# Spare expert tiles read in place by register, half 1 routed ahead of the experts, and another order on ScalarE, GpSimd and VectorE

## The chip, the cores and the metric

The kernel runs on one core of one Trainium2 chip. The metric is the device time in microseconds (us) of one execution; its median over 3 runs was 405.51 (404.76 to 406.37). Engines are named PE (TensorE), DVE (VectorE), ACT (ScalarE), POOL (GpSimd) and SP (SyncE, which here only issues transfers).

## The reference

Input: x of 4 x 256 rows of 256 numbers, and a context of 4 x 256 rows of 64. Four blocks are added to x in turn, each gated by a tanh:

```python
x = x + tanh(g_xattn[0]) * attn0(layernorm(x), ctx)     # softmax over 256 of a normalised similarity
x = x + tanh(g_ffn[0])   * ffn0(layernorm(x))           # router: the best 1 of 32 experts per row
x = x + tanh(g_xattn[1]) * attn1(ctx, layernorm(x))     # sigmoid of the top 76 of 256, made symmetric
x = x + tanh(g_ffn[1])   * ffn1(layernorm(x))           # top 8 of 64 experts, and one shared expert
```

In ffn0 each of the 32 experts has one ternary weight matrix of 256 x 256, masked by its own 0/1 mask, and a row gets only the output of the expert that its router picked. In ffn1 all 64 experts are computed for all rows and weighted by a row of W that is zero outside the best 8.

## The kernel before

The 1024 rows lie as T = 8 tiles of 128 rows; tiles 0 to 3 are half 0, tiles 4 to 7 half 1. Each engine has its instructions written out by hand in one order, and semaphores tie them together. The order of those lists is what the change moves.

**attn0.** attend(h) on DVE adds the softmax rows to X and asks POOL for the roots of the variances (rsqrt(r), r counts the requests); norm_rows on ACT writes the normalised rows (f16 high part to rows16, f32 to XN) and low_rows on POOL the low part. router_x and router (PE) give the router's logits, choose (DVE) the expert of each row.

**ffn0, routed.** Rows are put into tiles of CAP = 32 rows of one expert: 32 own tiles, one for each expert, and SPARE = 15 spare tiles for experts with more than 32 rows in a half. ranks, owners and owners_of (PE) with assign_spares, assign_owners, assign_slots and set_owners (DVE) give every row its slot, and spare_e the expert of each spare tile. scatter(h) (POOL, 4 indirect transfers) sends the rows to memory, load_rows(h) (ACT's queue) reads them back in slot order. There are 12 groups of four tiles, in 6 pieces p. For a piece PE transposes (routed_x), ACT copies (routed_rows), PE multiplies (experts) with m16, the masked weights, that DVE makes in eight mask_weights; ACT copies the result (expert_rows) and stores it (store_rows). In experts the four tiles of a group have a column group of the array each: a matmul is 128 rows deep, 32 columns wide and streams 256. Pieces 4 and 5 are the spare tiles. Their weights are copies: load_spares(h) on SP reads an expert number into a register and moves 128 KB within the core's memory, 15 times a half.

gather(h) (POOL) brings each row's output back to Z, weigh_rows (ACT) multiplies by the router's weight wtop, which weights_of_rows(h) on DVE makes from router_exp(h) on ACT, and add_rows (POOL) adds to X.

**attn1.** The search for the 76 largest of each row of SIM runs on DVE the whole time: find(n) is n steps, each a MAX8 or a MATCH_REPLACE8, 19 steps a tile (need_of), strung in between all other DVE work. adjacency(t) follows the 19 steps of tile t and needs tanh_rows on ACT. symmetric(0, k) on PE makes the symmetric matrix of two tiles and needs both adjacencies. rows_stats and rows_ask(h) (DVE), rsqrt (POOL), rows_affine (DVE), mix_rows (ACT), rows_mix (DVE) and rows_moments (DVE) with another rsqrt lead to rows_normalise; prep_x3t transposes it on PE and prep_rows copies it on ACT.

**ffn1.** shared_step and then 2 x 32 passes of pair_step and down, each for two experts. SP loads the weights of pair q to one of two stages (load_pair, which waits until lo_ready says that the stage was read), high_half on ACT makes their f16 high part, low_half on POOL the low part. Pairs 0 to 7 are prepared ahead of the loop. keep_busy are fills: matmuls on ones whose result nobody reads.

The expression that the change replaces in experts is this one (lines 985 to 990):

```python
e = 4 * (2 * p + k) + j
w = m16[:, e, c, :] if e < E0 else wov[h][min(e - E0, SPARE - 1)][:, c, :]
last = mm(ps_y[p % 2][CAP * j:CAP * (j + 1), k * D:(k + 1) * D],
          xT[:, h, 2 * p + k, c, s, CAP * j:CAP * (j + 1)], w,
          start=(i == 0), stop=(i == 2 * C - 1), skip_group_check=True)
```

## Time and profile before

| | us |
|---|---|
| median of 3 runs | 405.51 |
| the profiled execution | 406.02 |
| its span, from first to last instruction | 404.3 |
| PE busy (of 2419 matmuls) | 358.7 |
| DVE busy | 272.6 |
| ACT busy | 181.1 |
| POOL busy | 163.0 |
| span up to the first shared projection | 123.4 |

Busy time is the time in which an engine works at something; its share says nothing of who waits for whom. The profile also lists who waited for whom, and the instructions of an engine in order of time: these are the views to read for a change of order.

### The profile page before, as it was taken

Reading aid. Unit: us, or ns where it says so; the run is one execution under the profiler, and the core shown is the slowest. Engines: PE = TensorE matmul, PEld = TensorE weight load, DVE = VectorE, ACT = ScalarE, POOL = GpSimd, SP = SyncE. Lnnn points to the kernel's source line nnn. Section 1 sums busy time; section 2 is a strip of 40 time slices with the busy share of each in tenths; the row PEclk is TensorE's granted clock in tenths of the full one; section 3 lists DMA queues with packets and bytes.
Section 4 is the critical chain, followed back from the end, with each engine's and each line's share of the span. In section 5 each row is a group of like instructions: output and inputs, shape, how many; then the busy total and the mean of one; then the engine's idle time right before and its main releaser. Section 6 shows DMA issues by size and latency. Waiting matters only on the chain. (4 is left out here: it accounts for less than half of the span.)

```text
span 404.3 us, 7694 instructions
## 1 busy us (share of the span) xinstructions
PE 358.7 (89%) x2419; PEld 217.4 (54%) x2419; DVE 272.6 (67%) x711; ACT 181.1 (45%) x354; POOL 163.0 (40%) x180
## 2 busy tenths in 40 slices
PE   8987928643977899999899999969999999999995
PEld 2755426312644365546466666645665656656563
DVE  3999896999376585999784484557555555555454
ACT  3477736624744446544645446533323233332331
POOL 6937542437551349978699677220000000000000
PEclk9996967785999899999999999999999999999999
DMA  7899964686701444445355442004121221212211
GB/s 186 139 258 218 197 208 149 221 263 217 233 17 51 128 137 131 130 131 195 132 190 174 159 153 73 25 29 146 61 78 58 72 71 58 78 56 74 77 53 52
DMA packets 50346, 51.31 MB, mean 127 GB/s; under 512 B 6732, under 2 KB 41484, under 8 KB 50318
## 3 DMA queue, kind: packets, MB, share of 16 engines
q1 hardware_dynamic: 34430, 38.08, 30.0%
q0 software_dynamic: 9216, 6.29, 9.1%
q10 hardware_dynamic: 6672, 6.59, 5.1%
q8 instruction: 14, 0.23, 0.2%
q14 instruction: 14, 0.11, 0.1%
HBM read 44.13 MB, written 7.08 MB: 127 GB/s over the span
## 5 line engine op out<-in xcount | busy, mean ns | idle before, releaser
L1047 PE MATMUL bank<-early,gu 128*128 128x512 f16 x768 | 177.7, 381 | 3.0 <-DVE arena L1608 3.0
L1047 PEld LDWEIGHTS bank<-early,gu 128*128 128x128 f16 (+1 forms) x768 | 75.0, 98 | 83.0 <-issue 4.4
L499 ACT ACTIVATE arena<-arena 128x512 f16<-128x512 f32 (+1 forms) x66 | 41.6, 631 | 134.6 <-DVE arena L1624 133.8
L1074 PE MATMUL bank<-dp,arena 128*128 128x256 f16 (+1 forms) x768 | 94.2, 273 | 1.1 <-POOL arena L457 0.7
L1074 PEld LDWEIGHTS bank<-dp,arena 128*128 128x128 f16 x768 | 74.7, 98 | 23.5 <-POOL arena L457 2.7
L1608 DVE TENSOR_TENSOR arena<-arena,bank 128x512 f32<-128x512 f32 x64 | 43.9, 686 | 56.7 <-PE bank L1047 40.2
L457 POOL TENSOR_TENSOR arena<-arena 128x512 f16<-128x512 f32 (+1 forms) x33 | 38.3, 1161 | 51.1 <-ACT arena L499 51.1
L1624 DVE TENSOR_TENSOR arena<-arena,early 128x512 f32<-128x512 f32 x64 | 48.4, 756 | 7.5 <-DVE arena L1608 2.7
L740 ACT ACTIVATE arena<-bank 128x512 f32<-128x512 f32 (+1 forms) x66 | 38.7, 588 | 17.5 <-PE bank L1047 17.4
L406 POOL TENSOR_TENSOR gu<-stage,gu 128x512 f16<-128x512 f32 x32 | 39.0, 1219 | 7.4 <-ACT dp L499 7.4
L1634 DVE TENSOR_TENSOR arena<-arena 128x512 f16<-128x512 f32 (+1 forms) x33 | 22.8, 691 | 24.5 <-ACT arena L499 24.5
L1206 DVE MAX8 t<-work 128x8 f32<-128x256 f32 x72 | 30.7, 426 | 2.0
L795 PE MATMUL bank<-ones 128*128 128x512 f16 x97 | 26.5, 420 | 1.8 <-DVE ones L1508 1.1
L407 POOL TENSOR_TENSOR dp<-stage,dp 128x256 f16<-128x256 f32 x32 | 27.5, 859 | 0.0
L1211 DVE MATCH_REPLACE8 work<-t,work 128x256 f32<-128x256 f32 x64 | 26.1, 408 | 0.0
L499 ACT ACTIVATE gu<-stage 128x512 f16<-128x512 f32 x32 | 19.7, 617 | 0.7 <-ACT arena L499 0.5
L975 PE MATMUL bank<-gu 128*32 128x256 f16 x256 | 12.0, 344 | 7.7 <-ACT gu L499 7.7
L795 PEld LDWEIGHTS bank<-ones 128*128 128x128 f16 x97 | 9.3, 104 | 16.0 <-issue 7.4
L499 ACT ACTIVATE arena<-bank 128x512 f32<-128x512 f32 (+1 forms) x18 | 10.7, 595 | 12.9 <-PE bank L975 7.0
L399 POOL TENSOR_TENSOR rstd<-var_in,minus_half 128x4 f32<-128x4 f32 x8 | 8.2, 1026 | 18.5 <-DVE var_in L1247 17.0
L1233 DVE BATCH_NORM_STATS2 bn<-X 128x6 f32<-128x256 f32 x32 | 11.8, 413 | 5.2 <-DMA X<-in_x 5.2
L420 POOL DMA_INDIRECT routed_rows<-arena,slot x8 | 10.1, 1265 | 8.9 <-DVE slot L1397 7.1
(184 smaller groups left out, 368.6 us busy)
## 6 DMA issues: line engine op xcount, KB each, us to landing
early<-token_weights SPq DMA_DIRECT2D x126, 128.0 KB, 2.9
stage<-in_gu_t SPq DMA_DIRECT2D x32, 256.0 KB
gu<-in_masks_t POOLq DMA_DIRECT2D x16, 256.0 KB, 22.5
stage<-in_dp_t SPq DMA_DIRECT2D x32, 128.0 KB
expert_rows<-arena ACTq DMA_DIRECT2D x12, 256.0 KB
dp<-gu SPq DMA_DIRECT2D x22, 128.0 KB, 2.3
routed_rows<-arena SPq DMA_DIRECT2D x1, 1536.0 KB, 17.5
arena<-routed_rows ACTq DMA_DIRECT2D x3, 512.0 KB, 5.1
```

The costliest lines, as they stand in the source:

```text
L406: nc.gpsimd.tensor_tensor(gu16[:, q, 1, :, :], stage_gu[s], gu16[:, q, 0, :, :], ALU.subtract)
L407: nc.gpsimd.tensor_tensor(dp16[:, q, 1, :], stage_dn[s], dp16[:, q, 0, :], ALU.subtract).then_inc(lo_ready, 1)
L457: nc.gpsimd.tensor_tensor(inter16[0:m, s, 1, :], inter[0:m, s, :], inter16[0:m, s, 0, :], ALU.subtract).then_inc(ilo_ready, 1)
L499: return nc.scalar.activation(dst, src, ACT.Copy, scale=scale)
L740: nc.scalar.activation(silu[0:m, s, :], ps_gate[s][0:m, :], ACT.Silu).then_inc(silu_ready, 1)
L795: mm(dst.rearrange("p (a b) -> p a b", a=4), ones16[:, :], ones16[:, None, :].to_broadcast([P, 4, P]), start=True, stop=True)
L1047: last = mm(dst[:, :], w, x16[:, h, b, c, :], start=(k == 0), stop=(k == 3 * C - 1))
L1074: last = mm(dst, inter16[0:m, s, a, k * P:(k + 1) * P], w, start=(q is None and j == 0 and k % 2 == 0), stop=True, skip_group_check=True)
L1206: last = steps(v.max(t8[:, t, :], src))
L1211: last = steps(v.match_replace(work[:, :], t8[:, t, :], src, NEG))
L1608: v.tensor_tensor(gated[0:m, s, :], silu[0:m, s, :], up, ALU.mult).then_inc(gated_ready, 1)
L1624: v.tensor_tensor(inter[0:m, s, :], gated[0:m, s, :], row, ALU.mult).then_inc(inter_ready, 1)
```

## The change

1. **Spare tiles.** load_spares and its copies are gone. PE loads the 15 expert numbers into registers (spare_owners(h)) and takes the weights from m16 at the register's address. The rows of a spare tile are laid so that a full 128-column slice holds its 32 columns at the tile's place and zeros elsewhere (DVE writes the zeros once at the start), and all four tiles of a group add up in one accumulation over full-width matmuls (experts_spare).
2. **Half 1 sooner.** The masks are applied behind attend(1); softmax_rows(1), router_x, router, router_rows(1) and norm_rows(1) stand ahead of half 0's experts; load_rows(1) and tanh_rows(0) stand behind store_rows(0, 3), and router_exp(1) behind half 0's last store.
3. **POOL.** rsqrt(4) follows add_rows at once, gather(1) follows low_half(4), rsqrt(5) stands ahead of low_half(7), and add_rows(4 to 7) ahead of the loop; on ACT weigh_rows(4 to 7) are ahead of prep_rows(0).
4. Fills and search steps are counted anew; statistics of half 1 stand three passes earlier in the loop.

Three places of the lists. DVE, behind set_owners of half 0. L1504 and L1524 are mask_weights, the TENSOR_TENSOR into gu. Before:

```order
L1406 COPY place<-idxf 128x4
L1504 TENSOR_TENSOR gu<-gu,tern 128x4x256 x12
L1316 ISA Z,tiny<-Z,beta_sb 128x256
```

and behind attend(1) in the changed kernel:

```order
L1267 TENSOR_SCALAR var_in<-mv 128x4
L1524 TENSOR_TENSOR gu<-gu,tern 128x4x256 x6
L1361 SCALAR_TENSOR_TENSOR nmr<-mv,rstd 128x4
L1524 TENSOR_TENSOR gu<-gu,tern 128x4x256 x6
L1369 COPY lg<-bank 128x128
L1372 MAX top<-lg 128x8 x4
```

The twelve instructions moved from ahead of the second softmax to between attend(1) and choose(1), whose first row is the COPY.

ACT, at the end of half 0's experts. Before, with router_exp(1) (L606) ahead of the copies of pieces 4 and 5:

```order
L634 DMA expert_rows<-arena 128x2x256 [waits y_copied]
L606 ACTIVATE lg,tiny<-lg,tiny,rstd 128x32 [waits max_ready]
L606 ACTIVATE lg,tiny<-lg,tiny,rstd 128x32 x3
L499 ACTIVATE arena<-bank 128x512 [waits y_ready]
L634 DMA expert_rows<-arena 128x2x256 [waits y_copied]
```

and now (L594 is router_exp):

```order
L635 DMA expert_rows<-arena 128x2x256 [waits y_copied]
L603 DMA early<-routed_rows 128x4x512 [waits row_out]
L603 DMA early<-routed_rows 128x4x512 x2
L641 ACTIVATE XN<-SIM 128x1024 [waits rows_ready]
L644 ACTIVATE XN<-XN 128x1024 [waits act_step]
L487 ACTIVATE arena<-bank 128x512 [waits y_ready]
L635 DMA expert_rows<-arena 128x2x256 [waits y_copied]
L487 ACTIVATE arena<-bank 128x512 [waits y_ready]
L635 DMA expert_rows<-arena 128x2x256 [waits y_copied]
L594 ACTIVATE lg,tiny<-lg,tiny,rstd 128x32 [waits max_ready]
L594 ACTIVATE lg,tiny<-lg,tiny,rstd 128x32 x3
```

The loads of half 1, both tanh passes and two copies now stand ahead of router_exp(1).

POOL, from the fifth root on, in the changed kernel (L386 root, L393 and L394 low_half, L416 gather):

```order
L386 TENSOR_TENSOR rstd<-var_in,minus_half 128x4 [waits var_ready]
L393 TENSOR_TENSOR gu<-stage,gu 128x512 [waits hi_ready]
L394 TENSOR_TENSOR dp<-stage,dp 128x256
L416 DMA Z<-expert_rows,slot 128x256 [waits y_out]
L416 DMA Z<-expert_rows,slot 128x256 x3
L393 TENSOR_TENSOR gu<-stage,gu 128x512 [waits hi_ready]
L394 TENSOR_TENSOR dp<-stage,dp 128x256
L393 TENSOR_TENSOR gu<-stage,gu 128x512 [waits hi_ready]
L394 TENSOR_TENSOR dp<-stage,dp 128x256
L386 TENSOR_TENSOR rstd<-var_in,minus_half 128x4 [waits var_ready]
```

Before, three low_half stood ahead of the first of these roots and one between the two, and the gather behind both.

The diff, cut:

```diff
 dp16 = sb("dp16", [P, PAIRS, 2, D], F16)
+spare_zero = dp16[:, PAIRS // 2:, :, :].rearrange("p a b c -> p (a b c)")
+spare_x = spare_zero.rearrange("p (k c s n) -> p k c s n", k=4, c=C, s=2)
+own_x = spare_zero.rearrange("p (a j n) -> p a j n", j=4, n=P)[:, :, :, 0:CAP]
...
 rows16 = arena[:, 0:4096].rearrange("p (k s n) -> p k s n", k=T, s=2)
-more = arena[:, 4096:8192].rearrange("p (j c o) -> p j c o", c=C, o=D)
-wov = [[dp16[:, PAIRS // 2 + j, :, :] for j in range(SPARE)],
-       [more[:, j, :, :] if j < 8 else dp16[:, j + 1, :, :] for j in range(SPARE)]]
...
-    def load_spares(h):
...
-        sp.wait_ge(owner_set, h + 1)
-        sp.wait_ge(mask_ready, MB)
-        for j in range(SPARE):
-            e = sp.value_load(spare_e[0:1, h, j:j + 1], min_val=0, max_val=E0 - 1)
-            sp.dma_start(wov[h][j], m16[:, bass.ds(e, 1), :, :].rearrange("p e c o -> p (e c) o")
-                         ).then_inc(wov_in[h], 16)
...
     load_pair(3)
-    load_spares(0)
-    load_pair(4)
-    load_pair(5)
-    load_spares(1)
-    for q in range(6, 8):
+    for q in range(4, 8):
...
         add_rows(t)
-    for q in range(4, 7):
-        low_half(q)
     rsqrt(4, HT)
+    low_half(4)
+    gather(1)
+    low_half(5)
+    low_half(6)
+    rsqrt(5, HT)
     low_half(7)
-    rsqrt(5, HT)
-    gather(1)
+    for t in range(HT, T):
+        add_rows(t)
...
         low_step(n, (n + 1) % 2)
-        if n == 10:
+        if n == 8:
             rsqrt(6, HT)
-        if 4 <= n < 4 + HT:
-            add_rows(n)
...
             act.wait_ge(y_ready, PIECES)
-        if q == 9:
+        if q == 10:
...
+    def spare_rows(h, p):
...
+        if h == 0:
+            act.wait_ge(spare_set, 1)
+        else:
+            act.wait_ge(y_ready, p + 1)
+        a = 4 * C * (p - E0 // 8)
+        copy(own_x[:, a:a + 4 * C, :, :], ps_xt[p % 2].rearrange("p (a j n) -> p a j n", j=4, n=CAP)
+             ).then_inc(xt_copied, 1)
...
         act.wait_ge(xt_ready, PIECES * h + p + 1)
+        if p >= E0 // 8:
+            spare_rows(h, p)
+            return
...
     scale_rows(1)
+    router_exp(0)
+    softmax_rows(1)
     sim1_rows(1, 0, 1)
-    router_exp(0)
     high_half(2)
-    tanh_rows(0)
...
     load_rows(0)
-    softmax_rows(1)
+    router_rows(1)
+    norm_rows(1, 4, 5, 6, 7)
...
     store_rows(0, 1)
-    router_rows(1)
-    norm_rows(1, 4, 5)
...
     store_rows(0, 2)
-    norm_rows(1, 6, 7)
...
     store_rows(0, 3)
-    router_exp(1)
+    load_rows(1)
+    tanh_rows(0)
...
     store_rows(0, 5)
+    router_exp(1)
...
     high_half(4)
-    high_half(5)
-    load_rows(1)
-    weigh_rows(0, 1, 2, 3)
...
     store_rows(1, 1)
+    weigh_rows(0, 1)
...
     store_rows(1, 2)
+    weigh_rows(2, 3)
...
     store_rows(1, 3)
-    high_half(6)
...
     store_rows(1, 5)
+    high_half(5)
+    high_half(6)
...
     high_half(7)
+    weigh_rows(4, 5, 6, 7)
...
             high_half(n + 4)
-        if n == 3:
-            weigh_rows(HT, HT + 1)
-        if n == 5:
-            weigh_rows(HT + 2, HT + 3)
-        if n == 6:
+        if n == 4:
             tanh_rows(1)
-        if n == 14:
+        if n == 12:
...
+    owner = []
...
+    def spare_owners(h):
...
+        pe.wait_ge(owner_set, h + 1)
+        owner[:] = [pe.value_load(spare_e[0:1, h, j:j + 1], min_val=0, max_val=E0 - 1) for j in range(SPARE)]
...
+    def experts_spare(h, p):
...
+        n = PIECES * h + p
+        pe.wait_ge(xt_copied, n + 1)
+        for k in range(2):
+            first = 2 * p + k - E0 // 4
+            for i in range(8 * C):
+                j, c, s = i // (2 * C), i // 2 % C, i % 2
+                e = owner[min(4 * first + j, SPARE - 1)]
+                last = mm(ps_y[p % 2][:, k * D:(k + 1) * D], spare_x[:, first, c, s, 96 * j:96 * j + P],
+                          m16[:, bass.ds(e, 1), c, :].rearrange("p e o -> p (e o)"),
+                          start=(i == 0), stop=(i == 8 * C - 1))
+        last.then_inc(y_ready, 1)
...
             pe.wait_ge(y_copied, n - 1)
-        if p == E0 // 8:
-            pe.wait_ge(wov_in[h], 16 * SPARE)
+        if p >= E0 // 8:
+            experts_spare(h, p)
+            return
...
                 for j in range(4):
-                    e = 4 * (2 * p + k) + j
-                    w = m16[:, e, c, :] if e < E0 else wov[h][min(e - E0, SPARE - 1)][:, c, :]
                     last = mm(ps_y[p % 2][CAP * j:CAP * (j + 1), k * D:(k + 1) * D],
-                              xT[:, h, 2 * p + k, c, s, CAP * j:CAP * (j + 1)], w,
+                              xT[:, h, 2 * p + k, c, s, CAP * j:CAP * (j + 1)], m16[:, 4 * (2 * p + k) + j, c, :],
...
     router(0)
-    sim1(1, 0, 1)
-    keep_busy(4, bank[0][:, :])
+    keep_busy(8, bank[0][:, :])
...
     owners_of(0)
-    keep_busy(36, bank[0][:, :])
+    sim1(1, 0, 1)
+    spare_owners(0)
+    keep_busy(20, bank[0][:, :])
+    router_x((2, 3))
+    keep_busy(4, bank[0][:, :])
+    router(1)
+    keep_busy(4, bank[0][:, :])
...
     routed_x(0, 2)
+    ranks(1)
...
     routed_x(0, 3)
-    router_x((2, 3))
+    owners(1)
...
     routed_x(0, 4)
-    router(1)
-    experts(0, 3, 0)
-    ranks(1)
-    experts(0, 3, 1)
+    owners_of(1)
+    experts(0, 3)
     routed_x(0, 5)
-    owners(1)
-    experts(0, 4, 0)
-    owners_of(1)
-    experts(0, 4, 1)
+    experts(0, 4)
     experts(0, 5)
+    spare_owners(1)
...
     experts(1, 5)
-    keep_busy(10, bank[0][:, :])
     symmetric(0, 0)
+    keep_busy(24, bank[0][:, :])
...
     v.memset(ones16[:, :], 1.0).then_inc(ones16_set, 1)
+    v.memset(spare_zero.bitcast(F32), 0.0).then_inc(spare_set, 1)
...
     choose(0)
-    find(2)
+    find(1)
...
     set_owners(0)
-    for m in range(2, MB):
-        mask_weights(m)
...
     weights_of_rows(0)
-    find(4)
+    find(6)
     attend(1)
+    for m in range(2, 5):
+        mask_weights(m)
+    attended(1)
+    for m in range(5, MB):
+        mask_weights(m)
+    choose(1)
     find(3)
-    attended(1)
-    find(6)
-    choose(1)
-    find(2)
...
         seen += 1
-    thresholds(HT * need_of - used[0] - 8)
+    thresholds(HT * need_of - used[0] - 20)
...
     rows_ask(0)
-    thresholds(2)
+    thresholds(4)
     rows_affine(0)
+    thresholds(10)
...
         find(4 if n in (2, 3, 4) or n > 8 else 3)
-        if 7 <= n < 7 + HT:
-            rows_stats(n - 3)
-        if n == 10:
+        if 4 <= n < 4 + HT:
+            rows_stats(n)
+        if n == 8:
             rows_ask(1)
-        if n == 13:
+        if n == 11:
```

## Rows read from the trace of the kernel before

**Rows 1.** The page: busy tenths of PE in 40 slices; the threshold search's MAX8
```profile
PE   8987928643977899999899999969999999999995
...
L1206 DVE MAX8 t<-work 128x8 f32<-128x256 f32 x72 | 30.7, 426 | 2.0
```

**Rows 2.** PE in order of time: start us, duration us, line, tiles, xcount, [idle before <-releaser]
```profile
97.89 1.90 PE L975 MATMUL bank<-gu 128*32 128x256 f16 x32 [6.25 <-ACT gu L499]
...
107.33 1.06 PE L975 MATMUL bank<-dp,gu 128*32 128x256 f16 x32 [0.22 <-ACT gu L499]
...
119.08 1.40 PE L1006 MATMUL bank<-ident,XN 128*128 128x128 f32 x8 [1.90 <-DVE XN L1283]
...
123.42 1.46 PE L1033 MATMUL bank<-early,shared 128*128 128x512 f16 x6
```

**Rows 3.** What DVE waited for: us in total, times, longest
```profile
DVE mix L1441 <- POOL rstd L399: 5.9, 1, 5.9
...
DVE lg L1349 <- PE bank L908: 3.7, 1, 3.7
...
DVE X L1452 <- PE bank L996: 2.0, 2, 1.1
...
DVE spares L1367 <- PE bank L925: 1.4, 1, 1.4
```

**Rows 4.** DVE in order of time, 44 to 78 us
```profile
44.20 11.02 DVE L1504 TENSOR_TENSOR gu<-gu,tern 128x1024 f16<-128x1024 f16 x12
...
62.81 0.08 DVE L1211 MATCH_VALUE_LOAD work<-t,work 128x8 f32 x1
...
70.92 0.29 DVE L1349 COPY lg<-bank 128x128 f32<-128x128 f32 x1 [3.68 <-PE bank L908]
...
77.27 0.17 DVE L1397 SCALAR_TENSOR_TENSOR slot<-place,rank_off 128x4 uint32<-128x4 f32 x1
```

**Rows 5.** PE in order of time, 35 to 71 us
```profile
35.05 3.75 PE L860 MATMUL bank<-early 64*128 64x256 f32 x8 [1.60 <-DVE Z L1307]
...
42.87 7.94 PE L795 MATMUL bank<-ones 128*128 128x512 f16 x36
...
65.10 0.61 PE L896 MATMUL bank<-ident,X 128*128 128x128 f32 x4
...
68.96 1.92 PE L908 MATMUL bank<-router_c,xn_t 128*128 128x32 f32 x16
```

**Rows 6.** Sequencers of SP and PE by line: duration ns min/median/max
```profile
L284 SPq TENSOR_LOAD <-spare_e x30: 13/273/957, 55.3 to 97.4; - x30
L284 SPq FUSED_REGOPS  x30: 5/152/177, 55.8 to 97.7; - x30
...
L1047 PEldq FUSED_REGOPS  x240: 46/46/60, 278.5 to 392.1; - x120
```

**Rows 7.** POOL in order of time, 77 to 111 us
```profile
77.72 1.03 POOL L420 DMA_INDIRECT routed_rows<-arena,slot  x1 [3.43 <-DVE slot L1397]
...
100.70 1.16 POOL L406 TENSOR_TENSOR gu<-stage,gu 128x512 f16<-128x512 f32 x1
...
109.83 1.05 POOL L399 TENSOR_TENSOR rstd<-var_in,minus_half 128x4 f32<-128x4 f32 x1
```

**Rows 8.** ACT in order of time, 44 to 78 us
```profile
44.70 1.05 ACT L640 ACTIVATE XN<-SIM 128x1024 f32<-128x1024 f32 x1
...
52.60 1.52 ACTq L615 DMA_DIRECT2D arena<-routed_rows  x3
...
77.18 0.40 ACT L606 ACTIVATE lg<-lg,tiny,rstd 128x32 f32<-128x32 f32 x1
```

**Rows 9.** PE's idle times within the first passes of the pair loop
```profile
174.61 2.75 PE L1047 MATMUL bank<-early,gu 128*128 128x512 f16 x12 [0.33 <-DVE arena L1608]
...
182.03 1.48 PE L1074 MATMUL bank<-dp,arena 128*128 128x256 f16 x12 [0.69 <-POOL arena L457]
...
196.69 2.75 PE L1047 MATMUL bank<-early,gu 128*128 128x512 f16 x12 [1.37 <-DVE arena L1608]
```

3 lines of the change are left out of this document (1 added, 2 removed).

## The prediction

> **What bounds the kernel now.** I read the page first. Its busy tenths of PE [rows 1] fall into two parts: from slice 14 on (some 138 us) PE is at 9 almost without a break, in 66 passes of the pair loop; before that it is often at 3 to 7. So time can be won in the first 123 us, ahead of the first pass, and in the few idle times within the passes. The last row of PE ahead of the loop is the shared projection at 123.42; it needs the transposes at 119.08, and those waited for DVE's XN [rows 2]. Following DVE back, its waits [rows 3] name what it stood for: 5.91 us for GpSimd's fifth root (mix), 3.68 for the second router logits (lg), 1.98 for the symmetric tiles, 1.40 for the first ranks. Their sum is 12.97 us. Apart from these DVE worked without a pause from 38.8 to 117, mostly in the threshold search; half 0's last adjacency, and through it the symmetric tiles, need all of its 76 search steps of four tiles. I call this DVE's line: both kernels do the same DVE work between 38.8 and the transposes, so the transposes move by what the idle time changes. PE's wait of 6.25 at 97.89 [rows 2] is not on that line: ACT stood in front of gathered rows, and half 1's experts still ended at 108.4, ahead of the need.
>
> **The early part.** Ranks of half 0 no longer stand behind sim1 and its fills, so most of the 1.40 goes (0.4 stays), and one search step fewer stands ahead (0.45, a MAX8 [rows 1]): DVE is free at 42.75 where it was at 44.20 [rows 4]. Then come the rows of the second softmax, search and attend(1), which filled 55.2 to 62.8 [rows 4]: 7.6, with two more search steps, 8.6; then six masks, 11.02 [rows 4]. DVE reaches the choice of half 1 at 42.75 + 8.6 + 11.0 + 0.1 = 62.5, where it was at 70.92 [rows 4]: 8.4 sooner.
>
> **The register loads.** Nothing in this trace loads a register on PE. The nearest row is SP's: a load 0.273 at the median and 0.152 of register work behind it [rows 6], with a check of 0.02 some 0.443, fifteen of them 6.6 us. Below, PE's sequencer can run ahead of the array: its 240 register operations in the loop cost 46 ns each [rows 6] and PE shows no idle time for them, which would make the loads free. Above, SP's longest load was 0.957 [rows 6], 1.13 with the rest, so fifteen take 17 us. I take 6.6, half of it beside sim1 where sim1 stands in front, and all of it in the open for half 1. So for half 0: sim1 starts at 41.3 and takes 3.75 [rows 5], to 45.1; the loads end near 50.4; 20 fills at 0.22 each (36 took 7.94 [rows 5]), some of them at half clock, take 6.0, to 56.4; two transposes with their copies and the second router took 65.10 to 70.88 with expert work between [rows 5], 5.1 without it: logits at 61.5. That is 1.0 ahead of DVE's need at 62.5, so the wait of 3.68 goes. **This is the first place where it can turn**: each us later than 62.5 is a us of DVE.
>
> **Slots of half 1.** From the choice to the slots took 70.92 to 77.4 [rows 4], 6.5. One search step more (0.5), ranks behind the first experts (0.45) and 0.2 at the owners make 7.65: slots at 70.2, 7.2 sooner. Idle 0.65.
>
> **The new wait on DVE.** This speaks against the change. DVE takes the weights of half 1 right behind its owners, near 71.3, and for that it needs router_exp(1). ACT now does that behind load_rows(1) (which waits for the scatter), tanh_rows(0) and the last two expert copies. From the slots: 0.3 to the start of the scatter; four issues near 1.0 with 0.3 between and the last end, 5.0 [rows 7]; 1.5 until ACT sees them (the first scatter ended at 51.1, its loads went out at 52.60 [rows 8]); 1.52 for three load issues; 2.1 for two passes like the 1.05 one; 1.15 for two copies with stores; 1.65 for four exponentials of 0.40 [rows 8]. That is 13.2: 83.4, and DVE waits 12.1 us. Nothing else is behind it but the search, which is what the end needs. So idle time becomes 0.4 + 0.65 + 12.1 + 0.95 (one symmetric tile pair) = 14.1 where it was 12.97: **+1.1 us**. GpSimd's 5.91 [rows 3] does vanish: the root no longer waits for a weight half (109.83 [rows 7] against a request at 103.6), and ten search steps stand where DVE stood. The gain and the new wait nearly cancel.
>
> **ACT ahead of the transposed rows.** weigh_rows(4 to 7) now stand in front of prep_rows(0), behind high_half(7), whose stage is free only when GpSimd has done low_half(5), and that is behind the second gather. From the fifth request: root 1.05, low_half(4) 1.75 (100.70 to 102.45), gather 4.9 as the scatter, low_half(5) 1.75 [rows 7], the load 3.5 (estimate), high_half 1.0, four weighings 1.8: 15.8. DVE's way from the same request to the first transposes is 1.95 + 0.5 + 5.35 + 0.95 + 0.9 + 3.9 = 13.55, and 0.7 more to their copy, 14.25. So ACT is **1.5 us** late; 0 at the low end, with a load of 2 us, and 2.5 at the high end. mix_rows(0) behind high_half(6) costs another 0.2.
>
> **Spare tiles.** A piece of 32 matmuls in four column tiles took 1.06 us [rows 2]. Full width they stream 256 columns one after another; twelve of 512 columns take 2.75 in a pass [rows 9], 0.11 for 256, so 3.6 us, 2.5 more for each of two pieces a half. Half 0's end stays ahead of ACT's scatter wait (cost 0); half 1's experts end near 105.3 instead of 108.4, its rows are out near 109.7, just when GpSimd is done with low_half(4): cost 0, with no slack. The Trainium skill (TensorEngine Tiling (Array Packing), Theoretical Speedup) gives a dimension of at most 32 up to a factor of 4, which speaks against giving up the tiles. By it a piece would take 4.2 us, half 1 would end 1.4 later and the whole would be 1.4 us more than my sum; the trace shows 3.4 (3.6 against 1.06), so it agrees in direction and stays under the page's bound. The removed transfers appear in none of DVE's waits [rows 3]: 0. The memset fits into DVE's first wait for x: 0.
>
> **The loop.** The idle times of 0.33 and 0.69 [rows 9] came in passes where DVE had statistics on top of four searches, and GpSimd had add_rows and the root; both move to lighter places or ahead of the loop: **-1.0**, between 0 and -2.6. The 1.37 stands behind mix_rows(1) on ACT and only moves with it.
>
> **The sum.** +1.1 + 1.5 + 0.2 - 1.0 = +1.8 us. The profiled execution took 406.02, so 407.8; the median of the runs is 0.5 below it, which gives **407.3 us**. About 0.5% (2 us) is what a measurement of this kernel can tell from no change.
>
> **The rivals.** (1) Slower: PE's register loads don't run beside sim1. They then end at 51.7, the array has been idle so long that more fills go at half clock (7.3), logits come at 64.1. The choice is 1.6 late and the later steps on PE 1.2: +2.8 on my sum, 410. Were a load as long as SP's longest, logits would be at 74 and the time near 419. It decides as soon as the loads end after 51.5. For it: the long load in [rows 6]. Against: PE hides its register work in the loop. Chance 0.18. (2) Slower: half 1's experts end late, because loads, fills and full-width pieces add up, and the fifth normalisation's root, now behind gather(1) on GpSimd, waits for it. Each us after 109.7 costs one: with 3 us, 410. For it: the gather starts with no slack in my working; against: ACT may be through sooner, as I count the loads in full. Chance 0.11. (3) Faster: the new wait is shorter (scatter and landing 1.5 less), the stage of pair 7 lands in 2 us, and all three idle times in the loop go (-1.6): 1.8 - 1.5 - 1.5 - 1.6 = -2.8, 402.7. For it: DVE stands still while GpSimd writes the scatter, and the root has no weight half in front. Against: each of the three must come true. Chance 0.21. My forecast has 0.50.
>
> **The numbers.** Range 402.5 to 412.5, from rival 3 to a little beyond rivals 1 and 2; about a tenth is left out on either side (above, the long register load). My own case reaches from 405 to 409.5, and three tenths of it are over 2 us slower: 0.15, with both slower rivals 0.44. Rival 3 gives 0.20 for faster by over 0.5%, a little of it ending within. That leaves 0.36 for within.
>
> **What would show it.** DVE waiting some 12 us for ACT's router_exp at the reciprocal behind the owners; no wait for logits or for the fifth root; transposes of XN between 119 and 122; ACT's copy of them behind weigh_rows; spare pieces near 3.6 us; no idle 0.69 in the loop. I am wrong if that DVE wait is under 9 us, if PE's loads take over 8 us or under 2, or if the first shared projection is ahead of 123.

## The result, and the profile after

| | kernel before | changed kernel | ratio, with its 95% interval |
|---|---|---|---|
| timed first | 405.94 (404.76 to 406.8) | 418.9 (418.38 to 420.86) | 1.0314 [1.0256, 1.0371] |
| once more, on another chip | 408.85 (405.35 to 411.63, 24 runs) | 414.38 (413.13 to 417.04, 9 runs) | 1.0125 [1.0089, 1.0162] |

The change is slower: by 3.1% where it was timed first, by 1.2% where it was timed beside its variants. Both agree in direction and disagree in size. All variants below are ratios to the kernel before, timed beside them, and so belong with the second row. The kernel before varies there by some 1.5% from run to run, so differences under half a per cent are read from traces, not from times.

Below are the trace of the first timing (span 419.1) and that of the repeat (span 411.3). First the busy tenths and clock of the changed kernel's page:

```profile
PE   8896668919967889999999999969999999999995
...
PEclk9969569968978889999999999978999999999999
```

A slice is 10.5 us here and 10.1 in the kernel before. Counted from 1, PE is steadily at 9 from slice 16 on (157 us), in [rows 1] from slice 15 (141 us). Ahead of it the clock is below 9 in slices 3, 5, 6, 9, 10 and 12 to 15, and then once more in slices 27 and 28 (272 to 293 us), around the turn of the halves. What DVE waited for from 39 to 132 us, first timing and then repeat (36 to 130 us):

```profile
DVE tiny L1432 <- ACT lg L594: 13.6, 1, 13.6
DVE X L1472 <- PE bank L1014: 3.2, 1, 3.2
DVE lg L1369 <- PE bank L906: 2.2, 1, 2.2
DVE spares L1387 <- PE bank L923: 1.6, 2, 1.4
```

```profile
DVE tiny L1432 <- ACT lg L594: 12.7, 1, 12.7
DVE lg L1369 <- PE bank L906: 2.1, 1, 2.1
DVE spares L1387 <- PE bank L923: 1.6, 2, 1.4
DVE X L1472 <- issue: 1.6, 1, 1.6
DVE bn L1253 <- POOL X L438: 0.6, 1, 0.6
```

Against [rows 3]: the 5.9 us for GpSimd's root are gone, 12.7 to 13.6 us for half 1's router exponentials on ACT have come, the wait for logits shrank but did not go. PE in order of time, first timing:

```profile
47.48 1.91 PE L858 MATMUL bank<-early 64*128 64x256 f32 x4
56.34 3.88 PE L793 MATMUL bank<-ones 128*128 128x512 f16 x9 [6.95 <-issue]
...
76.68 7.15 PE L952 MATMUL bank<-gu,dp 128*128 x64
92.28 3.59 PE L793 MATMUL bank<-ones 128*128 128x512 f16 x8 [8.45 <-issue]
...
132.02 0.66 PE L1024 MATMUL bank<-ident,XN 128*128 128x128 f32 x4 [1.85 <-DVE XN L1303]
...
138.12 2.45 PE L1051 MATMUL bank<-early,shared 128*128 128x512 f16 x6 [1.22 <-DVE early L1484]
```

The two idle times of 6.95 and 8.45 us are the register loads. The transposes stand at 132.02 (119.08 in [rows 2]) and the shared projection at 138.12 (123.42), at half clock: 2.45 us for what took 1.46. The sequencer's loads for half 0:

```profile
L941 PEldq TENSOR_LOAD <-spare_e x15: 293/301/493, 46.4 to 55.7; - x15
L941 PEldq FUSED_REGOPS  x15: 146/146/165, 47.0 to 56.1; - x15
```

From the first to the last there are 9.3 us over 14 steps: 0.66 us each, although load, register work and check last 0.465 together.

**The start.** Of the 12.9 us at the transposes, 3.6 stood already at the choice of half 0: 41.7 (38.1 before). PE had waited for a transfer that both kernels issue, and the clock fell behind it:

```profile
18.10 0.63 PE L840 MATMUL bank<-router_sb,mean_w 128*128 128x32 f32 x4 [1.83 <-DMA router_sb<-in_router_t]
```

```profile
20.00:24.00 4.00, 4.00 (x11) 2.67 (x10) 2.02 (x5) 1.30 (x3) 0.45 (x1) 0.50 1.26 255
```

(The second view is the windows view, from 20 to 24 us; the granted clock is the third number from the end: 0.50, that is 1.2 GHz.) The repeat has no wait there, full clock, and its choice at 38.7, with the new memset ahead of it as in the first timing. The kernel before isn't spared either: with an edit to its last part alone (the turn's fills, below) its choice stood at 41.1, also behind a stretch at clock 0.50. I therefore count from the choice of half 0:

| us after the choice of half 0 | before | repeat | difference |
|---|---|---|---|
| logits of half 1 read | 32.8 | 25.2 | -7.6 |
| first request for the mixed rows' root | 65.3 | 70.7 | +5.4 |
| fourth adjacency of half 0 | 66.4 | 78.7 | +12.3 |
| transposes | 80.9 | 86.5 | +5.6 |
| first product of the loop | 86.6 | 93.1 | +6.5 |
| turn of the halves (transposes of half 1's token weights) | 229.2 | 233.4 | +4.2 |
| end of the span | 366.2 | 372.6 | +6.4 |

So the prologue loses 6.5 us, the loop up to the turn gains 2.3, and 2.2 are lost again behind the turn. Each column is one execution.

### The profile page after: what moved, and what is told of

Its sections match the earlier page's. It is cut to its first block and busy times, and to the rows that moved or that the text cites. A ratio compares the mean times of both kernels' runs of the same rounds, so it can differ in the third digit from the quotient of the medians.

```text
span 419.1 us, 7711 instructions
## 1 busy us (share of the span) xinstructions
PE 376.4 (90%) x2429; PEld 232.2 (55%) x2429; DVE 277.8 (66%) x712; ACT 181.3 (43%) x354; POOL 161.5 (39%) x180
## 5 line engine op out<-in xcount | busy, mean ns | idle before, releaser
L1092 PE MATMUL bank<-dp,arena 128*128 128x256 f16 (+1 forms) x768 | 95.5, 275 | 0.4 <-DVE arena L1656 0.4
L1092 PEld LDWEIGHTS bank<-dp,arena 128*128 128x128 f16 x768 | 75.7, 99 | 22.8 <-DVE arena L1656 0.7
L1646 DVE TENSOR_TENSOR arena<-arena,early 128x512 f32<-128x512 f32 x64 | 46.3, 724 | 7.6 <-DVE arena L1630 2.7
L793 PE MATMUL bank<-ones 128*128 128x512 f16 x107 | 32.7, 464 | 16.5 <-issue 15.4
L742 ACT ACTIVATE arena<-bank 128x512 f32<-128x512 f32 (+1 forms) x66 | 38.7, 588 | 18.6 <-PE bank L1065 18.5
L393 POOL TENSOR_TENSOR gu<-stage,gu 128x512 f16<-128x512 f32 x32 | 38.2, 1194 | 1.2 <-ACT dp L487 1.1
L793 PEld LDWEIGHTS bank<-ones 128*128 128x128 f16 x107 | 11.6, 115 | 32.6 <-issue 25.0
L394 POOL TENSOR_TENSOR dp<-stage,dp 128x256 f16<-128x256 f32 x32 | 28.9, 902 | 0.0
L386 POOL TENSOR_TENSOR rstd<-var_in,minus_half 128x4 f32<-128x4 f32 x8 | 8.6, 1074 | 19.5 <-DVE var_in L1267 14.4
L487 ACT ACTIVATE arena<-bank 128x512 f32<-128x512 f32 (+1 forms) x18 | 10.7, 595 | 10.5 <-PE bank L952 4.7
L952 PE MATMUL bank<-gu,dp 128*128 x128 | 14.3, 273 | 0.4 <-ACT dp L487 0.4
L952 PEld LDWEIGHTS bank<-gu,dp 128*128 128x128 f16 x128 | 12.4, 98 | 2.0 <-issue 0.6
L380 POOL DMA_DIRECT2D gu<-in_masks_t x16 | 12.2, 836 | 2.3 <-DMA X<-in_x 2.3
```

The costliest lines, as they stand in the source:

```text
L393: nc.gpsimd.tensor_tensor(gu16[:, q, 1, :, :], stage_gu[s], gu16[:, q, 0, :, :], ALU.subtract)
L394: nc.gpsimd.tensor_tensor(dp16[:, q, 1, :], stage_dn[s], dp16[:, q, 0, :], ALU.subtract).then_inc(lo_ready, 1)
L487: return nc.scalar.activation(dst, src, ACT.Copy, scale=scale)
L742: nc.scalar.activation(silu[0:m, s, :], ps_gate[s][0:m, :], ACT.Silu).then_inc(silu_ready, 1)
L793: mm(dst.rearrange("p (a b) -> p a b", a=4), ones16[:, :], ones16[:, None, :].to_broadcast([P, 4, P]), start=True, stop=True)
L952: last = mm(ps_y[p % 2][:, k * D:(k + 1) * D], spare_x[:, first, c, s, 96 * j:96 * j + P], m16[:, bass.ds(e, 1), c, :].rearrange("p e o -> ...
```

## The experiments

The theory behind them: DVE's idle time ahead of half 0's fourth adjacency is the loss, and two edits cause it, the exponentials' place on ACT and the register loads. The rivals: the loads alone, the clock, the spare pieces, the early part. Theory A and rival B are each run's own, as its expectation names them.

**The changed kernel again** (the repeat; no edit).

> The changed kernel once more, unedited, beside the others of this call. The five traces of its edits show the first choice of experts 37.5 to 38.8 us after the start four times and 45.7 once, where its own trace had 41.7 and the kernel before 38.1. Theory A (the 3.5 us that it had lost by then are chance, TensorE's clock at half speed between 20 and 28 us in that one execution): this trace has it at 37.5 to 39 and a span 2 to 4 us under 419.1, a ratio of 1.02 to 1.03. Rival B (the zeroing or the transfers make it systematic): 41 us or later again.

Ratio 1.0125, choice at 38.7: theory A for the start, the 3 us were that execution's. The other runs of the first timing had spans 2 to 5 us shorter, 414.2 to 417.3; those of the repeat have 411.3 to 415.0, so the two overlap a little and the first timing stays higher. The two traces are further apart than the medians: the first timing's is of its longest execution, the repeat's of its shortest. The traces show where most of it arose: counted from the choice, the fourth adjacency is the same (78.9 and 78.7), but from there to the transposes the first timing took 11.4 us and the repeat 7.8. In the first timing that adjacency ran beside GpSimd's weight halves (1.53 us for 0.51), and TensorE then made the second pair of symmetric tiles at half clock; first timing, then repeat:

```profile
122.20 1.22 PE L1011 MATMUL bank<-SIM,ident 128*128 128x256 f32 x2 [3.50 <-DVE SIM L1249]
```

```profile
118.26 0.59 PE L1011 MATMUL bank<-SIM,ident 128*128 128x256 f32 x2
```

Why GpSimd's and VectorE's work meet there in one execution and not in the other is not settled.

**Exponentials first** (e1).

```diff
-            store_rows(0, 5)
-            router_exp(1)
+            store_rows(0, 5)
...
+            router_exp(1)
             load_rows(1)
```

> The changed kernel with one step moved on ScalarE: the exponentials of half 1's router stand ahead of the loads of half 1's rows and of tanh, not behind the last expert copies of half 0. Theory A (VectorE's 13.6 us wait for these exponentials is what set the end of half 0's prologue): the wait shrinks below 3 us, the thresholds run through without it, the first request of a root of the mixed rows is then held by GpSimd's row additions (108.7 in the changed kernel's trace) rather than at 112.6, and the time falls by about 4 us, 418.9 to some 415. Rival B (the register loads and slower expert pieces on TensorE set the end): the wait goes and the time falls by less than 1 us, since the first transposes of the next block still wait for the same releaser.

1.012 [1.0028, 1.0212]: nothing gained against 1.0125. DVE's waits (36 to 125 us):

```profile
DVE SIM L1249 <- ACT XN L644: 7.8, 1, 7.8
DVE lg L1369 <- PE bank L906: 4.1, 1, 4.1
DVE tiny L1432 <- ACT lg L594: 2.8, 1, 2.8
```

The wait fell from 12.7 to 2.8 and the next one took its place: the first adjacency now stood 7.8 us for tanh, which is still behind the loads of half 1's rows. The fourth adjacency came 1.4 us earlier than in the repeat (77.3 after the choice), the transposes 0.9 later. The expectation's 4 us were set against 418.9 and missed. The trace is of the longest of four executions.

**One register load for each half** (e2).

```diff
-owner[:] = [pe.value_load(spare_e[0:1, h, j:j + 1], ...) for j in range(SPARE)]
+owner[:] = [pe.value_load(spare_e[0:1, h, 0:1], ...)] * SPARE
```

> The changed kernel with one register load for each half instead of 15: all spare tiles take the weights of the first spare tile's expert (rows of the other spare tiles are multiplied with a wrong expert's weights), the work stays the same size. Theory A: TensorE's idle of 7.0 and 8.5 us shrinks by 14 x 0.465 = 6.5 us each; but VectorE still waits for ScalarE's exponentials, which stand behind half 1's scatter, and all of that moves forward by 6.5 us, so that the time falls by 5 to 6.5 us to some 413. Rival B (the loads were beside other waits): less than 2 us.

This leaves out fourteen loads of each half; the rows of those tiles get a wrong expert's weights.

1.012 [1.0043, 1.0197]: in the times again nothing, where 5 to 6.5 us were expected. In the trace the logits came 3 us earlier, the root's request 3.8 (66.9 after the choice) and the fourth adjacency 3.9 (74.8), but the transposes only 0.5 (86.0): as in the first timing, the adjacency ran beside GpSimd's weight halves and the second symmetric pair at half clock.

**Both** (e3).

> Both edits at once, the exponentials first and one register load for each half (spare tiles take the first one's expert). If the two act on one chain in turn: some 409 to 411, still over the kernel before by the 3 us that the changed kernel had lost by its 40th us. If the loads alone matter: as with one load alone. If neither: 417 to 419.

1.0003 [0.9964, 1.0042]: both together give the whole loss back. Why the times show nothing of either alone is less clear. On VectorE's line the edits nearly add up:

| against the repeat, us after the choice | exponentials first | one load | both |
|---|---|---|---|
| fourth adjacency | -1.4 | -3.9 | -6.0 |
| from there to the transposes (repeat: 7.8) | 10.1 | 11.2 | 11.4 |
| transposes | +0.9 | -0.5 | -2.4 |

All three lost some 3 us again between adjacency and transposes, as the first timing did (11.4). Against that trace, with the same stretch, they are 2.9, 4.3 and 6.2 ahead at the transposes. The intervals of the single edits leave room for 3 us. The profiled execution with both was also spared at the turn (136.9 us to the end, 139.2 in the repeat), which the edits did not aim at; at the turn it was still 2.0 behind the kernel before. So the two edits are the cause together, and how much each is worth in time is not shown. The waits left (36 to 125 us):

```profile
DVE SIM L1249 <- ACT XN L644: 6.7, 1, 6.7
DVE X L1472 <- PE bank L1014: 3.2, 1, 3.2
DVE tiny L1432 <- ACT lg L594: 2.9, 1, 2.9
```

**Loads spread** (e5) over the pieces, 7 + 2 + 2 + 2 + 2, nothing left out.

```diff
             routed_x(0, 1)
+            spare_owners(0, 0, 7)
             experts(0, 0)
+            spare_owners(0, 7, 9)
```

> The changed kernel, nothing left out, with its 15 register loads for each half spread over TensorE's program: 7 behind the transposes of the half's second piece, where TensorE waits for ScalarE anyway (3.6 and 3.1 us in the trace with one load), and 2 behind each of the first four pieces' matmuls. Theory A (the price of the loads lies in where they stand, as 7 us of an idle array in one block): as with one load for each half, 413 +- 1.5 us. Rival B (every load stops the array wherever it stands, and what is behind it is late by 0.465 us): no gain, 417 to 419, with idle time of about 0.9 us behind each of the first four pieces.

1.0211 [1.0124, 1.0298] from few and scattered runs, the profiled one with its choice at 45.7: neither expectation is borne out. For the loads the trace is of use. The 7 loads hide in a wait for ACT (3.83 us; with one load and the exponentials first it was 3.61). Behind them come four pairs of loads, and the array stands for two of them:

```profile
70.34 1.90 PE L995 MATMUL bank<-gu 128*32 128x256 f16 x32 [3.83 <-ACT gu L487]
72.17 1.03 PE L972 MATMUL bank<-ident,arena 128*128 128x128 f16 x8
...
76.11 1.06 PE L995 MATMUL bank<-gu 128*32 128x256 f16 x32
77.95 0.61 PE L972 MATMUL bank<-ident,arena 128*128 128x128 f16 x8 [0.78 <-issue]
...
80.44 0.62 PE L972 MATMUL bank<-ident,arena 128*128 128x128 f16 x8 [0.79 <-ACT dp L487]
```

Behind 32 matmuls at half clock (1.90 us) a pair of loads left no gap, and neither did the next pair (behind 29 such matmuls, 1.87 us). Behind the same 32 at full clock (1.06 us) a pair left 0.78 and 0.79. So a load runs beside matmuls that were issued ahead of it, and the array stands for what exceeds them. The end gained nothing (transposes 88.1 after the choice, 86.5 in the repeat): DVE now waited 14.1 us for the exponentials.

**Exponentials and tanh first** (e6; tanh_rows(0) also ahead of load_rows(1)).

> The changed kernel with both of ScalarE's steps for VectorE ahead of the loads of half 1's rows: the exponentials of half 1's router and half 0's tanh. The trace with the exponentials alone moved shows VectorE waiting next at the first adjacency, 6.7 us, for this tanh. Theory A (VectorE's line sets the end of the prologue and each wait on it counts until the next one): 413.8 (exponentials alone) falls by another 2 to 4 us, to 410 to 412; the last adjacency comes 3 to 6 us earlier. Rival B (the row additions on GpSimd are the bound by then): 413 to 414.

1.0196 [1.0094, 1.0297]: theory A not borne out. The tanh wait fell to 1.7, but the exponentials' rose to 7.4 again: they stood behind four expert copies, and ACT stood still for 3.72 us ahead of the fourth, for which the profile names no engine of this core. Behind that DVE stood 4.6 us for GpSimd's row additions, the wait that rival B named. The idle time of ACT is not in the trace with the exponentials alone first (there they ended 38.6 us after the choice, here 43.4), so this run is no clean test of its edit.

**Order, loads and thresholds together** (e7: e5 + e6, 16 thresholds behind the statistics where 20 were).

> The changed kernel, nothing left out, with three edits that the runs so far name: exponentials and tanh ahead of the loads of half 1's rows on ScalarE, the register loads spread over the pieces, and 4 of the 20 thresholds that stand behind the first statistics put ahead of them (16 and 6 in place of 20 and 10). Theory A (VectorE's idle time before the fourth adjacency, 17 us in the changed kernel against 5 in the kernel before, is the loss): the fourth adjacency comes 66 to 70 us after the choice, not 79, the transposes 80 to 83, not 90, and the time is 407 to 410. Rival B (each edit only uncovers the next wait, as tanh first did): 412 to 416.

1.0047 [1.0006, 1.0088], 411.35 us where 407 to 410 were expected. In the times most of the loss is repaired. In the trace the fourth adjacency is at 73.1 after the choice and the transposes at 84.6, 1.9 of the 5.6 us lost, and both missed what was expected (66 to 70, 80 to 83). 7.9 us of wait for the exponentials are left, and one that the change itself brought: its 24 fills between the two pairs of symmetric products now stand in front of the second pair, which VectorE waits for.

```profile
113.42 5.34 PE L793 MATMUL bank<-ones 128*128 128x512 f16 x24
118.60 0.59 PE L1013 MATMUL bank<-SIM,ident 128*128 128x256 f32 x2
```

```profile
DVE X L1482 <- issue: 3.9, 1, 3.9
```

The adjacency was done at 114.7. No run took these fills out.

**Exponentials earliest** (e16; with e7's edits and the fills of e11, below).

```diff
             store_rows(0, 1)
+            router_exp(1)
             expert_rows(0, 2)
```

> The mended changed kernel of e15, with half 1's exponentials three copies earlier on ScalarE, behind the copy of half 0's second expert piece (some 68 to 70 us, when their maxima have been there since 64), not behind the fourth. Theory A (the copies and the waits for expert pieces ahead of them are what VectorE waits for): the wait falls from 7.9 to under 1 us, the first statistics are held by GpSimd's row additions, the fourth adjacency comes 3 to 6 us earlier, and the ratio is 0.99 to 1.0 where it was 1.0054. Rival B (the additions of the rows are the bound already): the ratio stays at 1.003 to 1.007 and the wait moves to the first statistics in full.

0.9988 [0.9945, 1.0031]; against 1.0054 without this edit (e15). The wait for the exponentials is gone from the list; the one for tanh is now 4.4. The fourth adjacency came 4.1 us earlier (69.5 for 73.6), the transposes 3.9. Theory A. At the turn (229.4 after the choice) and at the end (366.5) the trace stands within 0.3 us of the kernel before's, although the 24 fills still cost some 3 us here. Nothing is left out in this version: it is the changed kernel repaired, but the fills at the turn are in it and not in the kernel before, and they alone are worth up to 1% there.

**In place alone, in the old order** (e8).

> The kernel before with the spare tiles alone changed (weights read in place by register, zeros around the rows, SyncE's copies gone), in the old order: half 0's 15 loads stand where 28 of the 36 fills stood, half 1's ahead of the 8 fills before its pieces, both ahead of waits. Theory A (in place is free where its loads stand in front of a wait, and costs where they don't: it is the new order that put them on the path): 405 to 408, no change against before. Rival B (the loads, the 3.5 us zeroing or the two pieces of 3.6 us for 1.06 us cost wherever they stand): 411 or more, with the last expert piece later by 5 us.

1.0106 [1.0032, 1.018]: rival B in the main. The root's request is where it was (64.9 after the choice), the transposes 3.5 later. The loads hid in the waits for the gathered rows in both halves. The place is the last spare pieces (span 411.1):

```profile
104.18 7.15 PE L954 MATMUL bank<-gu,dp 128*128 x64
...
113.33 0.59 PE L1013 MATMUL bank<-SIM,ident 128*128 128x256 f32 x2
```

Half 1's experts end at 111.2 instead of 108.4 (3.4 later counted from the choice, where 5 were expected), and the symmetric products stand behind them (110.49 before).

**The order alone, spare tiles copied by SP as before** (e12).

> The changed kernel's order with the spare tiles as before: SyncE copies the spare weights, the pieces of spare tiles are 1.06 us again, no register loads on TensorE, no zeroing. If the loss lies in the order (ScalarE's exponentials for half 1 behind half 1's scatter): VectorE still waits 12 to 14 us for them and the time is within 2 us of the changed kernel's, 411 to 414 where the changed kernel has 414.4. If it lies in the spare tiles in place: no more than the kernel before, 406 to 409. By the terms so far (register loads 7 us ahead of half 1's router, of which one load alone gave back some 4 relative to the choice): 409 to 412, that is, both parts count.

1.0371 [1.0298, 1.0443]: the worst of all, by neither expectation. PE, then DVE, then SP's queue (36 to 132 us):

```profile
85.14 3.60 PE L973 MATMUL bank<-dp,gu 128*32 128x256 f16 x64 [14.51 <-DMA dp<-gu]
```

```profile
DVE tiny L1410 <- ACT lg L607: 21.1, 1, 21.1
```

```profile
SPq L282 <- DVE gu L1502: 23.0, 1, 23.0
```

SP's copies need all masked weights, and in the new order DVE makes most masks after the next half's attention: the copies are 23 us late, PE waits 14.5 for them, and the exponentials behind those expert copies 21.1. The new order needs the tiles in place; the parts do not add up.

**The loop's part alone** (e4) on the kernel before.

> The kernel before with only the loop's part of the change: ScalarE's weighting and GpSimd's adding of tiles 4 to 7 ahead of the loop, statistics, root, mix and tanh of half 1 two to three passes earlier. By the traces the changed kernel's passes up to the 23rd start 3.90 us apart all through, where the kernel before had 0.33, 0.69 and 1.37 us of TensorE idle three times, some 3 us in all. If that gain stands alone: 403 +- 1 us. If the earlier weighting and adding is paid for ahead of the loop, or the clock takes the gain back at the turn of the halves: 405 to 407.

1.0068 [1.0023, 1.0112]. The passes are even, but the weighting of tiles 4 to 7 stood on ACT in front of the copies that PE needs; ACT, then PE:

```profile
120.89 0.51 ACT L499 ACTIVATE Z<-Z,tiny 128x256 f32<-128x256 f32 x1 [6.84 <-DMA Z<-expert_rows,slot]
```

```profile
126.83 3.68 PE L1012 MATMUL bank<-gate_sb,xn_t 128*128 128x65 f32 x16 [6.01 <-ACT xn_t L499]
```

**With the weighting behind prep_rows(0)** (e9):

> The kernel before with the loop's part of the change, but the weighting of tiles 4 to 7 behind the preparation of the next block's rows on ScalarE, not ahead of it. The trace of the loop's part alone shows ScalarE waiting 6.8 us for the gathered rows at 114 to 125 with the copies that TensorE waits for (6.0 us idle) behind them, and the matmuls after that at half clock. Theory A: this wait is the whole loss and the loop's gain stands: 403 to 405 against 409.5 with the weighting ahead and some 406 to 407.6 for the kernel before. Rival B (the loop's gain is nothing): 407 +- 1.

0.9974 [0.9926, 1.0023]: the 6 us wait is gone, the gain over the kernel before too small to tell. 1.5 us are still paid ahead of the loop: TensorE stands 2.75 us ahead of the transposes of half 0's token weights, where it stood 1.22.

**GpSimd's root first** (e10), on the kernel before.

```diff
-            for q in range(4, 7):
-                low_half(q)
+            low_half(4)
+            low_half(5)
             rsqrt(4, HT)
+            low_half(6)
             low_half(7)
...
+            mix_rows(0)
             expert_rows(1, 5)
...
-            keep_busy(10, bank[0][:, :])
             symmetric(0, 0)
```

> The kernel before with GpSimd's root alone: the root for half 0's mixed rows ahead of the low halves of pairs 6 and 7 (it stood behind pair 6, 5.9 us of VectorE's time at the mix), ScalarE's mix ahead of the copy of the last expert piece, and the 10 fills before the symmetric products gone. Theory A (with the root in time, the symmetric products behind the last expert piece at 108.4 are the bound, 2.1 us earlier than they stood): the mix of the rows 2 to 3 us earlier, transposes at 116 to 117 in place of 119.1, time 403 to 404.5 against 406 to 407.5. Rival B (the clock falls without the fills and takes it back): 406 to 408.

0.9951 [0.9911, 0.999]. DVE's 5.9 us for the root became 5.5 us for the symmetric products; what was won is the 1.7 us by which these come earlier (70.7 after the choice for 72.4; transposes 79.4 for 80.9).

**Fills at the turn** (e11), on the kernel before.

```diff
                 if n == NS - 1:
+                    keep_busy(12, bank[1][:, :])
                     prep_wt(1)
```

> The kernel before with 12 fills (some 2.6 us) ahead of the transposes of half 1's token weights, where TensorE is idle for 3.20 us in every trace so far. After this same gap the matmuls ran at half clock in some executions and not in others: from the start of these transposes to the end there are 137.0 and 136.9 us in two traces and 138.3 to 140.7 in seven. Theory A: the fills hold the clock, the last stretch takes 137.0 in every execution, and the median falls by 1 to 2 us. Rival B: the fills change nothing, or delay the transposes: within 0.3% of the kernel before.

0.9896 [0.983, 0.9962], from four runs. The turn in the changed kernel, first timing, and then with fills:

```profile
279.33 1.12 PE L1041 MATMUL bank<-ident,Z 128*65 128x128 f32 x4 [3.20 <-DVE Z L1516]
280.24 2.77 PE L1092 MATMUL bank<-dp,arena 128*128 128x256 f16 x12
282.80 2.67 PE L1051 MATMUL bank<-early,shared 128*128 128x512 f16 x6
```

```profile
267.48 2.75 PE L795 MATMUL bank<-ones 128*128 128x512 f16 x12
270.85 0.65 PE L1023 MATMUL bank<-ident,Z 128*65 128x128 f32 x4 [0.61 <-DVE Z L1497]
271.33 1.47 PE L1074 MATMUL bank<-dp,arena 128*128 128x256 f16 x12
272.64 1.46 PE L1033 MATMUL bank<-early,shared 128*128 128x512 f16 x6
```

All fourteen traces without these fills have the same idle 3.20 us; in two of them (one is the kernel before's) the clock stayed and the rest took 136.9 us, in twelve it fell and the rest took 138.3 to 140.7. All six with fills took 136.9 or 137.0.

**What can be had together.** e14 is root and fills; e13 has the loop's part too, with the weightings in two idle times of ACT; e15 is e7 with the fills; e17 is e13 with 6 fills ahead of the first token weights.

> The kernel before with the turn's fills and the root first, without the loop's part: 0.984 to 0.988 if the two add up.

0.9912 [0.9869, 0.9956], where 0.984 to 0.988 were expected.

> The kernel before with the turn's fills, the root first (as in the run with the root alone), and the loop's earlier steps, with the weighting of tiles 4 and 5 behind the preparation of rows and that of tiles 6 and 7 behind the top experts' exponentials, where ScalarE had 2 us of idle time. If the three add up (1.0%, 0.5%, and the loop's 2 us without the 1.6 us that the weighting cost): ratio 0.977 to 0.985, some 400 to 402 us. If the loop's part gives nothing: 0.984 to 0.99, as without it.

0.9882 [0.9841, 0.9922], 404.07 us beside 408.64: faster than both kernels, though not by the 0.977 to 0.985 expected, so the gains do not add up in full. The times of e13 and e14 can't be told apart. In their traces the loop's part is worth something: from the first product to the turn e13 takes 142.0 us, e14 144.0 and the kernel before 142.6.

> The changed kernel with its waits mended (exponentials and tanh first, loads spread, 16 thresholds) and the turn's fills. Without the fills its trace has 139.8 us from the turn to the end. With them 137: a ratio of 0.995 to 1.0, where it was 1.0047 [1.0006, 1.0088]. If the turn's clock is not the matter: 1.003 to 1.006.

1.0054 [1.0009, 1.01]: from the turn to the end it took 136.9 us, as expected (139.8 without the fills), and the ratio did not fall (1.0047 without them). So what the fills are worth in time lies between nothing here and 1% on the kernel before, and is not settled.

> The version with all good parts (0.9882) with 6 fills more (1.3 us) ahead of the transposes of half 0's token weights, where TensorE was idle for 2.63 us and then ran at half clock for some 8 us. Theory A (the fills hold the clock there too): 2 us more, a ratio of 0.983 to 0.985, the first 12 products of the loop 2.75 us in place of 4.64. Rival B: no difference, 0.988 +- 0.002.

0.9885 [0.9804, 0.9966]: rival B. The transposes ran at full clock, but the loop's first 12 products still took 5.28 us, behind another idle time of 1.26.

## Why the prediction was wrong

The direction of its likeliest case was right, the time (407.3, range to 412.5) not: 418.9, or 1.0125 on the repeat where 407.3 is 1.0044. The repeat's ratio on this kernel's 405.9 would be 411.0, which is inside the range and 3.7 over the forecast. The step that failed is the price of the register loads: 0.443 us each, 6.6 for fifteen, of which 3.3 in the open and no wait for half 1's logits. They took 0.66 each, 9.9 in all, 7.0 to 7.9 of it in the open, and the logits came 2.1 us too late. By the steps of the prediction, with the repeat's trace:

- **DVE's line** as the frame held: the transposes moved by +5.6 us, DVE's idle time between choice and transposes from 12.97 to 18.6, the same +5.6. That its work is the same held only in sum: the twelve mask instructions took 7.4 us instead of 11.0, and attend(1) 3.95 instead of 1.67. In the kernel before eleven of the masks stood 0.6 us apart, beside GpSimd's scatter; the twelfth took 4.4, beside GpSimd's weight halves. It is attend(1) that now stands beside these. The last two masks of the kernel before, and the first weight half:

```profile
50.22 5.00 DVE L1504 TENSOR_TENSOR gu<-gu,tern 128x1024 f16<-128x1024 f16 x2
```

```profile
51.15 1.17 POOL L406 TENSOR_TENSOR gu<-stage,gu 128x512 f16<-128x512 f32 x1
```

- **The new wait** for router_exp(1): 12.1 predicted, 12.7 and 13.6 measured. Right, place and size.
- **The register loads: the step that failed.** The load was priced at 0.443 by its duration on SP; it takes 0.66 from one to the next. 15 took 9.9 us, not 6.6; what lay beside sim1 was 3, as assumed, so 7.0 to 7.9 were open and not 3.3. (The prediction's end of the loads at 50.4 does not follow from its own terms, which give 45.1 + 3.3 = 48.4; the repeat's ended at 53.3.) The logits were 2.1 us late at DVE: they came 1.8 later than forecast, and DVE was there 1.3 sooner, since its masks took less; the forecast had 1.0 of slack. That is the outcome of rival 1, which had a chance of 0.18, but not its mechanism: the loads did run beside sim1, and each cost more. The Trainium skill (DMA: Bandwidth & Descriptors, Latency and other measured facts) gives a floor of some 600 ns for a tensor_load. The trace agrees in the distance from one to the next (0.66), not in the duration that it shows (0.30). By that floor fifteen loads would take at least 9.0 us, an estimate, 2.4 more than the sum had.
- **The other waits:** ranks 1.6 for 1.05, symmetric products 1.6 to 3.2 for 0.95, row additions 0.6 for none. With the logits and the new wait that makes idle time +5.6 and not +1.1. This term was mis-sized by 4.5 us; the logits are the largest part of it.
- **ACT ahead of the transposed rows:** +1.5 predicted; PE waited 1.47 for the copy where it had 0.45: +1.0. In the first timing none of it, DVE being later still.
- **The loop:** -1.0 predicted, -2.3 measured: all passes up to the 23rd were 3.90 us apart, and the 0.69 is gone.
- **Spare pieces:** 3.6 predicted, 3.58 measured. The cost 0 was wrong where they stand alone (in place alone, in the old order: half 1's experts ended 2.8 later, and DVE waited 5.4 us for the symmetric products instead of 2.0); here the later DVE hid it. A piece is 3.4 times as long as in column tiles (3.58 against 1.06). The working has a slip: 4.24 less 3.6, for two pieces, is 1.3 and not 1.4.
- **Not in the sum:** the clock. 2.2 us behind the turn, where the one trace of before had been spared; in the first timing also 3.6 at the start and 3.6 between the fourth adjacency and the transposes. A single trace showed these gaps without their price.
- **Rivals 2 and 3:** rival 2 needs half 1's rows to be out after 109.7. They were out at 114.8, 5.1 later, but the root behind them was asked only at 122.9 and began 0.4 later, so this was not the bound. Rival 3 did not happen; its part in the loop did.

The sum in the repeat, from the choice on: +5.6 (DVE) + 0.9 (ACT) - 2.3 (loop) + 2.2 (turn) = +6.4. The median difference is 5.5, but that they are near is no test: the sum compares two single executions. The 2.2 of the turn rest on a trace of before that was spared there, as the kernel before's other variants without fills were not, and the first timing's loss between adjacency and transposes, which other traces of the changed order share, is not in it.

## What to carry to other kernels

Price an instruction of a sequencer by the distance from one to the next, not by its duration, and put register loads behind matmuls that last as long as they do, or in front of a wait that is there anyway. When work is moved on one engine, move what other engines wait for with it: here the exponentials (three copies earlier) and the loads. Where one such repair shows nothing in the times, look at the next fixed event on the engine that sets the pace, here the fourth adjacency: it moved with each edit, while other losses behind it hid that. When something comes earlier, look at the fills as well: those counted for the old wait now stand in front of work. And an idle time of TensorE in one trace has no single price: the same 3.20 us here were followed by half clock in most traces and by full clock in two. Fill it, or count it at both clocks.

## What was not expected of the hardware

- Register loads on TensorE take 0.66 us from one to the next, though each is shown with 0.30. They run beside matmuls issued ahead of them: two left no gap behind 32 matmuls that took 1.90 us, and one of 0.8 us behind 32 that took 1.06 (e5). Of fifteen ahead of the second router, 7 to 8 us were open.
- The same 3.20 us of idle TensorE was followed by half clock in twelve of fourteen traces and by full clock in two.
- DVE and GpSimd slow each other: four scalar_tensor_tensor of 256 columns took 3.95 us beside GpSimd's weight halves and 1.67 without, GpSimd's halves 0.84 and 1.33 for 0.67 and 1.16. One mask took 4.40 us beside them and 0.60 beside GpSimd's indirect transfers, which in turn took 1.40 to 1.61 for 0.96. The Trainium skill (SBUF — State Buffer, Who interferes with whom) says that a DVE instruction with two inputs in SBUF contends with a GpSimd instruction that reads SBUF. These traces agree; no run here took one of the two away.
- In the repeat and three variants (e5, e6, e7) half 0's first spare piece had gaps of up to 0.85 us that its waits don't explain, 2.5 us in all in the repeat and in e6, 1.4 in the others; in the first timing, with the exponentials first (e1) and with one load there were none. ACT had an idle time of 3.7 to 4.5 us near them in the repeat and in the same three, and one of 3.68 in the kernel before, for which the profile names no engine of this core either. This stays open.
